# First attention of a four-layer kernel: 64x64 tiles for maxima and values, four denominator sources, output scaling on GpSimd

## The reference

```python
q, k, v = the three parts of leaky(xn @ Wc.T + bc), per head
scores = q @ k.T * (1 / sqrt(8))
attn = softmax(scores)                    # over 1024 keys
out = leaky(concat_heads(attn @ v) @ Wo.T + bo) + xn
```

## Time and profile before

| | |
|---|---|
| time, median of 3 runs (lowest to highest) | 1097.56 us (1096.79 to 1098.14) |
| span of the profiled execution | 1097.5 us |
| time of that execution | not given apart from its span |
| instructions | 15954 |
| PE busy | 989.5 us (90%) |
| DVE busy | 791.0 us (72%) |
| POOL busy | 725.9 us (66%) |
| ACT busy | 556.4 us (51%) |
| mean granted TensorE clock | 0.954 of full |

### The profile page before, as it was taken

One profiled execution on the slowest core, in us unless ns is written; L12 is line 12 of the kernel. 1 busy time (PEld: TensorE's weight loads), 2 busy tenths in 40 slices (PEclk: granted clock), 3 DMA queues, 4 the chain that ended last, 5 costly groups with the idle time before them and its releaser, 6 DMA issues.

```text
span 1097.5 us, 15954 instructions
## 1 busy us (share of the span) xinstructions
PE 989.5 (90%) x5234; PEld 448.8 (41%) x5234; DVE 791.0 (72%) x1263; ACT 556.4 (51%) x927; POOL 725.9 (66%) x591
## 2 busy tenths in 40 slices
PE   5899998999999999999998998589996686789997
PEld 3347561222222222222221222389985432348795
DVE  5864768877778878887777831676489999996513
ACT  2474445665666565565565665334354323146362
POOL 5560507899988777999787999104438887874322
PEclk9899998999999999999999999889998897689999
DMA  9363523111110100111000110556771110054562
GB/s 327 104 193 108 154 64 100 29 34 46 40 39 21 52 21 27 44 31 55 28 21 26 38 33 22 171 157 211 245 225 44 53 31 27 1 159 121 154 186 77
DMA packets 91189, 96.52 MB, mean 88 GB/s; under 512 B 22380, under 2 KB 67436, under 8 KB 90852
## 3 DMA queue, kind: packets, MB, share of 16 engines
q1 hardware_dynamic: 77668, 84.73, 24.9%
q0 software_dynamic: 5120, 10.50, 3.2%
q10 hardware_dynamic: 8320, 0.26, 0.4%
HBM read 70.22 MB, written 24.77 MB: 87 GB/s over the span
## 4 chain that ended last, share of the span: by engine, by line
PE 62%; POOL 14%; DVE 11%; issue 4%; ACT 4%; DMA 2%; ACTq 1%; SPq 1%; POOLq 0%; DVEq 0%
PE ps L228 58%; POOL psum_sb L234 8%; PE ps L231 4%; ACT ar L271 2%; POOL ar L234 2%; DVE ar L234 2%; POOL xsort L288 2%; DVE ar L247 2%; DVE small L247 2%; ACTq L274 1%; DVE osb L247 1%; SPq L274 1%; DMA psum_sb<-in_L_bv 1%; DVE psum_sb L234 1%; ACT lrow L268 1%
## 5 line engine op out<-in xcount | busy, mean ns | idle before, releaser
L228 PE MATMUL ps<-ar 64*128 64x512 bf16 (+5 forms) x3264 | 591.9, 430 | 34.1 <-DVE ar L234 9.9
L271 ACT ACTIVATE ar<-ps 128x1024 f32<-128x1024 f32 (+2 forms) x336 | 302.8, 906 | 205.6 <-PE ps L228 197.6
L228 PEld LDWEIGHTS ps<-ar 128*128 128x128 f32 (+2 forms) x3264 | 238.3, 147 | 369.1 <-issue 300.7
L247 DVE TENSOR_REDUCE small<-ps 128x2 f32<-128x1024 f32 (+2 forms) x276 | 312.8, 1146 | 70.9 <-PE ps L228 69.7
L234 POOL TENSOR_TENSOR psum_sb<-psum_sb,ar 128x1024 f32<-128x1024 f32 x128 | 308.9, 2413 | 20.2 <-ACT ar L271 5.1
L234 POOL TENSOR_TENSOR ar<-ar 128x512 f32<-128x512 f32 (+1 forms) x80 | 106.2, 1331 | 38.0 <-DVE ar L247 20.0
L293 POOL DMA_INDIRECT gT<-ysort,rt x48 | 46.3, 965 | 96.8 <-issue 96.6
L234 POOL TENSOR_TENSOR psum_sb<-ar 128x1024 f32<-128x1024 f32 x32 | 75.4, 2357 | 33.8 <-ACT ar L271 32.0
L234 DVE TENSOR_TENSOR ar<-ps,ar 128x256 f32<-128x256 f32 (+4 forms) x56 | 56.4, 1011 | 50.1 <-PE ps L228 42.7
L268 ACT COPY ar<-ps 128x256 f32<-128x256 f32 (+1 forms) x84 | 30.6, 383 | 88.2 <-PE ps L228 60.3
L234 DVE TENSOR_TENSOR on_sb<-osb,rec_sb 128x512 f32<-128x512 f32 x32 | 55.5, 1734 | 22.4 <-DMA rec_sb<-lscr 22.3
(11 more groups left out here) (156 smaller groups left out, 1073.2 us busy)
## 6 DMA issues: line engine op xcount, KB each, us to landing
ar<-in_L_up SPq DMA_DIRECT2D x48, 384.0 KB, 4.1
ar<-in_L_b SPq DMA_DIRECT2D x32, 322.0 KB, 3.6
rec_sb<-lscr SPq DMA_DIRECT2D x64, 128.0 KB, 2.9
scr<-ar SPq DMA_DIRECT2D x48, 128.0 KB, 2.0
ar<-xsort SPq DMA_DIRECT2D x40, 128.0 KB, 3.7
ysort<-ar SPq DMA_DIRECT2D x40, 128.0 KB, 3.8
ar<-scr SPq DMA_DIRECT2D x32, 112.0 KB
xsort<-xs SPq DMA_DIRECT2D x12, 256.0 KB, 6.6
```

The lines of the kernel that those rows point to most:

```text
L228: return self.e.matmul(o, l, r, start=start, stop=stop) if self.e else Nothing()
L247: return self.e.tensor_reduce(o, a, AX.X, op, negate=True) if negate else self.e.tensor_reduce(o, a, AX.X, op)
L271: return self.e.activation(o, a, fn, **kw) if self.e else Nothing()
```

## The change

The maximum pair becomes four matmuls of 64 rows by 64 columns, and so does the value product, whose two row halves (keys 0 to 63 and 64 to 127 of a tile) now accumulate apart, in banks 6 and 7. ScalarE copies bank 6 to osb at k = 1, and VectorE adds bank 7 to it, also at k = 1. GpSimd stops after the add of step 4; the denominators are made at k = 1 from four sources (exponentials of step 5, the sum, exponentials of steps 6 and 7), in a slot of the ring, and ScalarE copies them at k = 2. The row maxima take a slot of the ring, too. The multiply of osb by rec_sb leaves VectorE's k = 11 and stands in GpSimd's program at step 3, behind its add; the last two are behind the loop and in a new `tail0`. The diff, without unchanged context:

```diff
     "gpsimd": (
-        "ln.1.2 ln.1.3 route.3 route.3 route.3 route.3 gather.2 gather.2 gather.2 gather.2 gather.2 gather.2 gather.2 "
+        "tail0 ln.1.2 ln.1.3 route.3 route.3 route.3 route.3 gather.2 gather.2 gather.2 gather.2 gather.2 gather.2 gather.2 "
...
 (TensorE, max_pair)
-                ins = pe.mm(ps[:, b, :], Qs[r, s, 2 * pr + a, 128 * qt:128 * qt + 128],
-                            Ks[r, s, pr, 512 * hk:512 * hk + 512])
+                for n in range(2):
+                    ins = pe.mm(ps[64 * n:64 * n + 64, b, :],
+                                Qs[r, s, 2 * pr + a, 128 * qt + 64 * n:128 * qt + 64 * n + 64],
+                                Ks[r, s, pr, 512 * hk:512 * hk + 512])
 (TensorE, pv)
-            b = 6 + (i // 8) % 2
             if kt == 0:
-                pe.wait_ge(*vacant(b))
+                pe.wait_ge(*vacant(6))
+                pe.wait_ge(*vacant(7))
             pe.wait_ge(*at("exp", i))
-            for a in range(2):
-                h = 4 * (g % 4) + 2 * pr + a
-                ins = pe.mm(ps[64 * a:64 * a + 64, b, :], V0[:, 1024 * tile + 64 * h:1024 * tile + 64 * h + 64],
-                            Ps[:, i % NP, 512 * a:512 * a + 512], start=kt == 0, stop=kt == 7)
-            ins.then_inc(*(filled(b, ("pvd", i)) if kt == 7 else up(("pvd", i))))
+            for n in range(2):
+                r = slice(64 * n, 64 * n + 64)
+                for a in range(2):
+                    h = 4 * (g % 4) + 2 * pr + a
+                    ins = pe.mm(ps[64 * a:64 * a + 64, 6 + n, :],
+                                V0[r, 1024 * tile + 64 * h:1024 * tile + 64 * h + 64],
+                                Ps[r, i % NP, 512 * a:512 * a + 512], start=kt == 0, stop=kt == 7)
+                if kt == 7:
+                    ins.then_inc(*filled(6 + n, ("pvd" if n else "pvd_low", i)))
+            if kt < 7:
+                ins.then_inc(*up(("pvd", i)))
 (TensorE, unit_tail)
-            b = 6 + u % 2
-            if k == 3:
+            if k == 1:
+                b = take(ring[0])
                 pe.wait_ge(*vacant(b))
                 pe.wait_ge(*at("exp", 8 * u + 7))
-                pe.wait_ge(*at("sums", u, 5))
-                for n, (r0, src) in enumerate(((0, Ps[:, (8 * u + 6) % NP, :]),
-                                               (64, psum_sb[:, 1024 * (u % 2):1024 * (u % 2) + 1024]),
-                                               (0, Ps[:, (8 * u + 7) % NP, :]))):
+                pe.wait_ge(*at("sums", u, 4))
+                for n, src in enumerate((Ps[:, (8 * u + 5) % NP, :],
+                                         psum_sb[:, 1024 * (u % 2):1024 * (u % 2) + 1024],
+                                         Ps[:, (8 * u + 6) % NP, :], Ps[:, (8 * u + 7) % NP, :])):
                     for a in range(2):
-                        r = r0 + 32 * a
+                        r = 64 * (n % 2) + 32 * a
                         ins = pe.mm(ps[r:r + 32, b, :], onesf[:, 0:32], src[:, 512 * a:512 * a + 512],
-                                    start=n < 2, stop=n > 0)
+                                    start=n < 2, stop=n > 1)
 (TensorE, attention)
-                    max_rows(rows_of(i, AFTER[i >= 16]), 6 + (i // 8 + 1) % 2)
+                    max_rows(rows_of(i, AFTER[i >= 16]), take(ring[0]))
 (VectorE, unit_tail)
+            if k == 1:
+                half = osb_[:, 512 * m:512 * m + 512]
+                dve.wait_ge(*at("osb_low", u))
+                dve.wait_ge(*at("pvd", 8 * u + 7))
+                dve.tt(half, half, ps[:, bank["pvd", 8 * u + 7], :], ALU.add).then_inc(
+                    *emptied(("pvd", 8 * u + 7), ("osb", u)))
...
-            if k == 11:
-                dve.wait_ge(*at(f"recip_in{m}", u))
-                dve.wait_ge(*at("osb", u))
-                if u >= 2:
-                    dve.wait_ge(*at("proj", u - 2))
-                half = slice(512 * m, 512 * m + 512)
-                dve.tt(on_sb[:, half], osb_[:, half], rec_sb[:, half], ALU.mult).then_inc(*up(("scaled", u)))
 (ScalarE, unit_tail)
-            if k == LAG:
-                act.wait_ge(*at("pvd", 8 * u + 7))
+            if k == 1:
+                act.wait_ge(*at("pvd_low", 8 * u + 7))
...
-            if k == 3:
+            if k == 2:
                 act.wait_ge(*at("sum", u))
 (ScalarE, attention)
-                    act.wait_ge(*(at("sums", u, max(k, 1)) if k <= 5 else at("sum", u)))
+                    act.wait_ge(*(at("sums", u, max(k, 1)) if k <= 4 else at("sum", u)))
 (GpSimd)
+        def scaled(x):
+            u = x // 8 - 2
+            if x % 8 != 3 or u < 0 or u >= 32:
+                return
+            half = slice(512 * (u % 2), 512 * (u % 2) + 512)
+            pool.wait_ge(*at(f"recip_in{u % 2}", u))
+            pool.wait_ge(*at("osb", u))
+            if u >= 2:
+                pool.wait_ge(*at("proj", u - 2))
+            pool.tt(on_sb[:, half], osb_[:, half], rec_sb[:, half], ALU.mult).then_inc(*up(("scaled", u)))
+
+        def tail0():
+            scaled(267)
+            yield
 (GpSimd, attention)
-                elif 2 <= k <= 5:
+                elif 2 <= k <= 4:
                     pool.wait_ge(*at("exp", i))
                     pool.wait_ge(*at("sums", u, k - 1))
                     pool.tt(a_, a_, Ps[:, i % NP, :], ALU.add).then_inc(*up(("sums", u, k)))
+                scaled(i)
                 if rows_of(i, 1):
                     max_rows(rows_of(i, 1))
                 yield
+            scaled(259)
```

More of the change, by code:

```diff
@@ L1769, in unit_tail @@
             m = u % 2
-            if k == LAG:
-                act.wait_ge(*at("pvd", 8 * u + 7))
+            if k == 1:
+                act.wait_ge(*at("pvd_low", 8 * u + 7))
                 if u >= 2:
                     act.wait_ge(*at("scaled", u - 2))
-                act.acp(osb_[:, 512 * m:512 * m + 512], ps[:, bank["pvd", 8 * u + 7], :]).then_inc(
-                    *emptied(("pvd", 8 * u + 7), ("osb", u)))
-            if k == 3:
+                act.acp(osb_[:, 512 * m:512 * m + 512], ps[:, bank["pvd_low", 8 * u + 7], :]).then_inc(
+                    *emptied(("pvd_low", 8 * u + 7), ("osb_low", u)))
+            if k == 2:
                 act.wait_ge(*at("sum", u))
@@ L2211, in pool_program @@
         weave(attention(), LANES_B, {"end0": end0, "ln": ln, "route": route, "gather": gather})
-        follow(ORDER_C["gpsimd"], {"ln": ln, "tile": tile, "route": route, "gather": gather})
+        follow(ORDER_C["gpsimd"], {"tail0": tail0, "ln": ln, "tile": tile, "route": route, "gather": gather})
     def sync_program(sp):
```

## The result

The changed kernel takes **1230.89 us** in the median of 4 runs (1229.69 to 1236.22), the kernel before 1097.22 in its own 4 (1096.79 to 1098.14): a ratio of **1.1215** with a 95% interval of 1.1181 to 1.1249. Slower, inside the range, 32 us over the forecast of 1199. The profiled execution took 1236.22 us with a span of 1234.4, the span of before being 1097.5; the mean granted clock of TensorE fell from 0.954 to 0.911.

The account below looks back on a forecast made before the run. TensorE was taken to bound each attention unit; the multiply's stall, +3.3 us per middle unit, with smaller terms summed to +102 on 1097.5, forecast 1199 us. The range was 1158 to 1236.

Parts of the forecast that it names:

- dearer multiply (+13): Upper end of the range: GpSimd's multiply at its dear end, +0.42 us in each of 30 units, 13 us.
- dearer tiles (+30): Upper end of the range: more tiles to start cost +0.2 us a step, 5 steps in 30 units, 30 us.
- rival A: Output product of step 4: TensorE stalls 2.65 us on GpSimd's multiply; 1199 us, chance 0.83.
- The timetable: One middle unit: multiply 370.09 to 371.39, output product at 371.49 instead of 367.92, next zero 380.37, +3.3 us a unit.
- The sum at full clock: Whole attention: +46.2, +36.1, +13.8, +4.5, +0.6 and +0.6 over its units, together +102 us on 1097.5.
- Unit 31: Last unit, from its zero to its denominators: 17.0 us instead of 12.5, +4.5.
- slower multiply at the very end: End of the attention: the last multiply is slower on GpSimd, +0.6 us.
- The clock: TensorE's 2.65 us pause in each unit was claimed not to lower its granted clock; nothing added.
- Tiles: Each step keeps two seams, 0.265 us; no saving taken, bounds -0.265 to +0.2 a step.
- Rival B: Tile seams in each step vanish though the scores stay 64x128: step 1.28 us, total 1160 us, chance 0.10.
- Ring and queue waits: Step 3's scores wait 0.55 us for the denominators' copy, step 4's maxima 0.35 for an exponential; both swallowed by the stall.
- Rival D: Output product of step 4: GpSimd in time, each add at 1.5 us; 1052 without seams, 1116 with; chance 0.04.

Follow-up runs that it names:

- experiment 1: Changed kernel with the multiply alone put back on VectorE at k = 11: 1185.75 us, ratio 1.0083.
- 3: Changed kernel with the multiply still on GpSimd, but ahead of the add of step 2: 1180.60 us, ratio 1.0046.
- 2: Kernel before with only the multiply moved to GpSimd behind the third add; old tiles, banks and denominators: 1272.37 us, ratio 1.0844.
- exp. 4: Changed kernel with three unused fp32 matmuls of 512 columns ahead of TensorE's wait for the multiply, units 0 to 27: 1272.74 us, ratio 1.0823.
- experiment 10: Changed kernel with one unused fp32 matmul (0.86 us) ahead of TensorE's wait for the multiply: 1269.10 us, ratio 1.0810.
- experiment 11: Changed kernel with one unused matmul of 256 columns ahead of TensorE's wait for the multiply, units 0 to 27: 1207.06 us, ratio 1.0973.
- experiment 5: Changed kernel with the multiply ahead of GpSimd's add of step 2, plus the scores as four 64x64 matmuls: 1081.72 us, ratio 0.9831.
- experiment 9: Kernel before with the maximum pairs alone as four 64x64 tiles: 1196.80 us, ratio 1.0184.
- 8: As experiment 5, with ScalarE's copy of the denominators moved ahead of the exponential of step 2: 1058.07 us, ratio 0.9618.

## Why the prediction was right and where it was wrong

In short: the stall is where the prediction put it and costs about what it said. The measured time lies inside its range partly by luck. The upper end was built from a dearer multiply (+13) and dearer tiles (+30), and neither came; a falling clock, priced at nothing, filled that room. The two terms on top of 1199 make 1242 and not the "about 1235" that was written; 1230.89 is inside either way.

**The multiply (rival A): right, shown from both sides.** Taken away it takes the wait with it (experiments 1 and 3), added alone to the kernel before it brings it (2). The timetable was right to 0.3 us at each point, the stall 2.47 instead of 2.65. The price of a multiply, 1.30 taken, is 1.266 in the mean.

**The sum at full clock: right, a little high.** Experiments 4 and 10 show what the order costs where the clock is kept:

| part | forecast | changed kernel | exp. 10 | exp. 4 |
|---|---|---|---|---|
| units 0 and 1 | +0.6 | +1.4 | +1.8 | +0.7 |
| units 2 to 15 | +46.2 | +59.7 | +40.8 | +42.5 |
| units 16 to 25 | +36.1 | +49.8 | +33.1 | +31.2 |
| units 26 to 30 | +13.8 | +20.8 | +15.4 | +12.8 |
| attention length | +96.7 | +131.7 | +91.1 | +87.2 |

(differences to the first profile of before; experiments 4 and 10 ran on the other kind of chip). A middle unit at full clock is 263.07 / 14 = 18.79 us, +2.9 and not +3.3. The product starts 0.3 earlier than forecast, and it and the five steps behind it take 1.06 and 7.60 us in experiment 10 (402.02 to 403.08 to 410.68), where 1.15 and 7.73 stood; the forecast's unit is 18.94 (361.43 to 380.37), the shorter ones of experiment 10 are 18.36, the others, with row transposes, mostly 19.13. Unit 31, forecast +4.5, came to +6.4, and of the +0.6 for a slower multiply at the very end nothing is seen.

**The clock: wrong.** The failing step is "After a pause of 2.9 us at 686.62 it is granted 1.00 and the denominators take their usual 1.84; I add nothing". It was one pause, once, and it was read as a rule. It was read wrong, too: 2.90 us is the length of the window, in which TensorE is busy for 0.60 us. The pause itself, in the kernel before, is 2.30 us:

```profile
689.52 0.62 PE L228 MATMUL ps<-ar,onesf 128*32 128x512 f32 x2 [2.30 <-POOL psum_sb L234]
```

So the row spoke for a shorter pause than the 2.65 us that it was to cover. In the changed kernel a pause of 2.46 or 2.47 us comes in nearly every middle unit, the clock falls in 11 of units 2 to 15, and the product takes anything from 1.10 to 2.05 us, by where the fall lands. Behind the longer pauses of the late units (2.8 to 4.6 us) it takes 2.04 to 2.08 every time from 642 us on in the first profile; in the second four of those nine take 1.32 to 1.76. The cost is 639.0 and 630.7 less the 594.4 and 598.4 of experiments 4 and 10: **32 to 45 us**, across two kinds of chip. On equal chips experiment 11, with 1.75 us of pause left, gives 23 us back; its units 2 to 15, all at full clock, take 262.74 us where those of the changed kernel's second profile take 282.52, so 20 us are the clock's in these units alone. The low stretches there last some 45 us together; half of that, less what falls into the pauses, comes to about the same (an estimate). The surplus over the forecast, 35 in the attention length and 32 in the medians, is this cost less the 6 to 10 us by which the sum at full clock was too high.

The Trainium skill, "TensorE: Matmul & The Clock Gate", Part 1 (The HAM clock gate), tells of a gate that grants 1.2 or 2.4 GHz by how busy the array has lately been, and of kernels that swing between the two. The windows of 0.50 and 1.00 here agree with its two levels and with the swinging (413.70 to 415.50 and 420.00 to 425.44 in the unit above).

**Tiles: right.** Two seams stayed, the step went from 1.545 to 1.52 us (421.18 less 420.86 is 0.32, and 1.20 follow). Rival B is false for the change as it is; experiment 5 shows what it would have taken, the scores in the same shape, which the change's short description (not printed here) names and the diff does not do. The Trainium skill, "TensorEngine Tiling (Array Packing)", section Tiling Modes, says that a change of mode drains the engine and a change of tile within a mode does not: the times of experiment 9 (a shape more, +0.125 us a step) and experiment 5 (one shape for all, -0.22) agree with both halves.

**Ring and queue waits: right in place, and of more weight than their sentence.** "Both are swallowed by the next item" holds for the changed kernel, where they last 0.40 and 0.30 us (0.55 and 0.35 were forecast). They are what is left of it without the stall (0.45 to 0.5 us a unit in 1 and 3), and the largest cost once the seams are gone (23.6 us between 5 and 8).

**Rival D, GpSimd in time: false, and its condition was not enough.** By the prediction's own timetable adds 2 and 3 start when the exponentials end (364.74 and 367.56), and in the changed kernel, too, they wait for ScalarE (1.00 and 0.34 us at 407.50 and 410.19). With adds of 1.5 us the multiply would by that timetable have come 0.85 us earlier, not 2.65. Nor did the adds come near 1.5 us; the fastest of 96 took 2.336:

```profile
L234 POOL TENSOR_TENSOR psum_sb<-psum_sb,ar x96: 2336/2347/2359, 172.4 to 817.2; 128x1024 f32<-128x1024 f32 x96
```

The spread of the earlier trace rows (to 2913 ns) is gone with VectorE's multiply. In experiment 1, where this multiply is back, its median is 682 ns (2058 before): it now starts mostly in GpSimd's short pause ahead of the third add (414.58 in the row above), and a third add that it overlaps takes 2.58 us (398.21). The undisturbed add times that the prediction took were right.

**What stays open.** Why the same pause of 2.47 us costs the clock in one unit and not in the next, and why 3.33 us could pass in experiment 10. One thing the rows do show: in six neighbouring units of the changed kernel the falls (273.4, 293.9, 314.3, 334.8, 355.3, 375.8) are evenly spaced, 20.5 us apart, while their products are 19.98 to 20.78 apart. Where in a unit the clock falls is thus not set by the pause alone. Open is also why the kernel before takes 77 us more on some chips. Between the nearly identical experiments 10 and 11, one on either kind, 37 us lie ahead of the first unit's zero (207.04 and 169.99) and 34 behind the last one's.

## What to carry to other kernels

An operation handed to an idler engine is priced by its place in that engine's queue, not by that engine's free time: the same GpSimd multiply costs 120 to 129 us behind the third add (639.0 and 630.7 against 510.25) and next to nothing ahead of the second. Where a stall like these (2.16 and 2.47 us) comes in every round of a loop on TensorE, add a clock term or a bound for it, even if one such pause in the trace went by unpunished, and read the pause from the engine's own row and not from the window around it. Tiles of one shape next to each other are what pays, so a change of shape is worth making for all neighbours or for none.

## What the chip showed that I had not expected

- A pause of 2.47 us, repeated about every 20 us, came with some 3.5 us at 1.2 GHz, sometimes 7, in 11 of the 14 units from 203 to 485 us (6.3 from 413.7 on in the unit shown); pauses of 1.33 (experiment 10) and 1.75 us (11) in the same place were followed by 1.00 in all middle units. Useless work that shortens the pause by 0.7 us made the kernel 23 us faster.
- A change of tile shape between neighbouring matmuls costs about 0.1 us, and four 64x64 tiles stream in about the time of two 64x128 (bf16, experiment 9) or two 128x64 (fp32: the step of experiment 5 is 1.29 us with two bf16 sets at 0.215 and 0.86 for the values).
- Two waits of half a microsecond for a copy and an exponential, invisible before, were worth 23.6 us once TensorE's steps had become shorter.
